# Graph attention and expert layers: part of the second stage's preparation moved into the attention's last slots

## What is computed

```
# x: 16 x 1024 x 256, adj: 16 x 1024 x 1024
Wh = layernorm(x) @ W.T;  e = leaky_relu(Wh@a1 [i] + Wh@a2 [j], 0.2), -inf where adj == 0
x1 = x + softmax(e) @ Wh
n  = layernorm(x1)
w  = softmax(mean_over_batch(n) @ Wr + br)          # per node, 8 experts
h  = relu(bn(n @ W1[e] + b1));  h = relu(bn(h @ W2[e] + b2))
out = x1 + sum_e w[:, e] * (h @ Wo[e] + bo[e])
```

## Time and profile before

| | us |
|---|---|
| median of 3 runs | 2882.55 (2881.88 to 2883.1) |
| the profiled execution | 2883.41 |
| its span, first to last instruction | 2881.6 |
| PE busy | 2809.0 (97%) |
| DVE busy | 2415.4 (84%) |
| ACT busy | 2133.3 (74%) |
| POOL busy | 685.5 (24%) |
| mean granted TensorE clock | 0.991 of full |

### The profile page before, as it was taken

One profiled execution on the slowest core, in us unless ns is written; L12 is line 12 of the kernel. 1 busy time (PEld: TensorE's weight loads), 2 busy tenths in 40 slices (PEclk: granted clock), 3 DMA queues, 4 the chain that ended last, 5 costly groups with the idle time before them and its releaser, 6 DMA issues.

```text
span 2881.6 us, 48960 instructions
## 1 busy us (share of the span) xinstructions
PE 2809.0 (97%) x17110; PEld 2482.4 (86%) x17110; DVE 2415.4 (84%) x3560; ACT 2133.3 (74%) x3035; POOL 685.5 (24%) x953
## 2 busy tenths in 40 slices
PE   7999999998999999999999999999999999999998
PEld 7989989988788888888888888888888888888887
DVE  7999999997688888888888888888888888888887
ACT  6889889887676777776777677677777777667775
POOL 5888888887000000000000000000000000000000
PEclk9999999999899999999999999999999999999999
DMA  4444444443344454554454444455455445544554
GB/s 144 158 154 149 154 154 155 148 158 110 105 172 151 159 161 159 159 165 156 157 163 159 154 159 163 148 168 162 151 168 161 154 158 162 161 152 160 157 156 136
DMA packets 159980, 445.25 MB, mean 155 GB/s; under 512 B 16016, under 2 KB 73784, under 8 KB 159808
## 3 DMA queue, kind: packets, MB, share of 16 engines
q1 hardware_dynamic: 159808, 442.96, 47.7%
HBM read 401.97 MB, written 40.93 MB: 154 GB/s over the span
## 4 chain that ended last, share of the span: by engine, by line
PE 73%; ACT 1%; DVE 1%; issue 0%; DMA 0%; ACTq 0%; DVEq 0%
PE z_ps L52 17%; PE z_ps L53 16%; PE z_ps L54 16%; PE m_ps L1012 7%; PE m_ps L1014 7%; PE m_ps L1015 7%; PE turn_ps L987 1%; PE turn_ps L995 1%; ACT h L1143 0%; PE m_ps L1029 0%; DVE h_lo L1304 0%; DVE h_sums L1311 0%; DMA gate_row<-w_scratch 0%; DVE h_lo L1316 0%; PE turn_ps L1103 0%
## 5 line engine op out<-in xcount | busy, mean ns | idle before, releaser
L1143 ACT ACTIVATE h<-z_ps,bn_shift,bn_scale 128x512 f32<-128x512 f32 x1024 | 748.5, 774 | 557.2 <-PE z_ps L54 333.2
L1304 DVE TENSOR_TENSOR h_lo<-h_sums,h_hi 128x1792 fp32r<-128x1792 f32 x256 | 519.4, 2029 | 208.5 <-ACT h_hi L1157 208.4
L1012 PE MATMUL m_ps<-h_hi,wo_ops 128*128 128x256 f32 x1792 | 513.3, 286 | 4.0 <-DVE h_lo L1304 4.0
L1015 PE MATMUL m_ps<-h_hi,wo_ops 128*128 128x256 f32 x1792 | 502.9, 281 | 0.0
L1014 PE MATMUL m_ps<-h_lo,wo_ops 128*128 128x256 f32 x1792 | 502.6, 280 | 0.0
L1157 ACT ACTIVATE h_hi<-h_sums 128x1792 fp32r<-128x1792 f32 x256 | 434.8, 1698 | 62.6 <-DVE h_sums L1327 59.9
L86 POOL TENSOR_TENSOR ffn_vareps<-ffn_mv,ln_eps 128x4 f32<-128x4 f32 x32 | 7.2, 224 | 1899.1 <-DVE ffn_mv L80 1899.1
L1311 DVE TENSOR_TENSOR h_sums<-h,gate_row 128x1024 f32<-128x1024 f32 x256 | 313.8, 1226 | 124.5 <-ACT h L1143 110.1
L52 PE MATMUL z_ps<-h_hi,w_hi 128*128 128x512 f32 x1024 | 405.8, 396 | 6.9 <-DVE h_lo L1316 6.9
L52 PE MATMUL z_ps<-xT_hi,w_hi 128*128 128x512 f32 x1024 | 407.7, 398 | 2.7 <-ACT h L1143 2.0
L53 PE MATMUL z_ps<-xT_lo,w_hi 128*128 128x512 f32 x1024 | 405.9, 396 | 0.0
(11 more groups left out here) (152 smaller groups left out, 5481.0 us busy)
## 6 DMA issues: line engine op xcount, KB each, us to landing
wo_ops<-wo_scratch SPq DMA_DIRECT2D x248, 896.0 KB, 6.3
adj_sb<-in_adj SPq DMA_DIRECT2D x128, 512.0 KB, 3.5
gate_row<-w_scratch SPq DMA_DIRECT2D x256, 256.0 KB, 4.5
x_sb<-in_x SPq DMA_DIRECT2D x64, 256.0 KB, 2.8
x_scratch<-x_sb SPq DMA_DIRECT2D x128, 128.0 KB, 1.8
ffn_x<-x_scratch SPq DMA_DIRECT2D x32, 512.0 KB, 7.5
out<-ffn_x SPq DMA_DIRECT2D x31, 512.0 KB, 8.0
...
```

What stands on the lines that cost most here:

```text
L1012: pe.matmul(m_at(q), w_hi, x_hi[:, x, :], start=e == 0 and q in OPENERS, stop=False, skip_group_check=True)
L1015: done = pe.matmul(m_at(q), w_lo, x_hi[:, x, :], start=False, stop=e == E - 1, skip_group_check=True)
L1143: return act.activation(dst, src, ACT.Relu, bias=bn_shift[layer][:, col], scale=bn_scale[layer][:, col])
L1304: dve.tensor_tensor(h2_lo[s % 2][:, :, :], g2[:, 1:8, :], bits(h2_hi[s % 2][:, :, :]), ALU.subtract) \
```

## The change

- Two Wo experts are loaded by SP in slot 8 of the last pair, ahead of the first tile's load. Their sums (DVE, slot 13) and expert 0's rounding and remainder are made in slots 13 and 14.
- Slot 12 (`GATE_SLOT`): TensorE transposes half of `node_table` (nodes 0 to 511) and the first row tile, ahead of the products of block 14; ACT copies and rounds them. Slot 14: logits of this half, z1(0), the softmax, the turned gates, ACT's copy, SP's store.
- The second half of the gates is made in the second stage: transposes at its start, logits between the layer groups of slot -2, softmax in DVE slots 0 and 1, `transpose_weights` at the end of PE slot 1, ACT's copy at the start of slot 2.
- The bias table comes in four parts, two matmuls each, in slots 4 to 7; `residual` moves to slots 9, 10, 14 and 15 for the first two tiles, and to slots 6 and 7 of its own tile afterwards (4 and 5 of the tile before, until now).
- Normalising of the second tile moves to slots 0 and 1, its transposes to 2 and 3. Experts 2 and on are summed and rounded in slots 0 and on.
- Buffers are shared to make room: wh, x and PSUM banks of the attention are read on by the second stage.

The diff, cut to this; `LastWeights` and `Gates` hold the old weight_sums, weight_upper, weight_lower and softmax as methods:

```diff
...
+        self.sums = [shared.x_rows[:, i * 4:(i + 1) * 4, :].rearrange("p s (h d) -> p (s h) d", d=P) for i in range(2)]
...
+    def home(self, e):
+
+        return (0, 0) if e == 0 else ((1, 2, 3)[(e - 1) % 3], (e - 1) // 3)
+
+    def load(self, sp, e):
+        i, _ = self.home(e)
+        for m in range(self.KB):
+            sp.dma_start(self.sums[i][:, (1 - m):4:2, :],
+                         self.Wo[e].rearrange("(k p) d -> p k d", p=P)[:, :, m * P:(m + 1) * P]) \
...
+    GATE_SLOT = UT - 4
...
+                if last and u == TB:
+                    sp.wait_ge(S["x1_ready"], (PAIRS - 1) * UT + TB)
+                    for e in range(2):
+                        last_w.load(sp, e)
...
+            sp.wait_ge(gates.wT_ready, 1)
+            sp.dma_start(w_dram[:, 0, :], first_tile.wT[0:E, :]).then_inc(first_tile.w_stored, DMA)
...
+                if last_pair and u == GATE_SLOT:
+                    pe.wait_ge(S["n1_added"], PAIRS * UT - CT + 1)
+                    pe.wait_ge(S["pT_lo_ready"], PAIRS * UT - 1)
+                    gates.transpose_rows(pe, lambda it, d: pT_ps[0][:, it * KB + d, :], feat_sum[:, 0:CT, :], ident)
+                    pe.wait_ge(norm.xn_ready, 1)
+                    for d in range(KB):
+                        for t in range(CT):
+                            last = pe.transpose(head_ps[:, d, t * P:(t + 1) * P], norm.xn[:, t, d * P:(d + 1) * P],
+                                                ident[:, :])
+                        last.then_inc(first_tile.xT_psum, 1)
...
+                if last_pair and u == GATE_SLOT + 2:
+                    pe.wait_ge(gates.featT_ready, 1)
+                    for it in range(CT):
+                        gates.row_logits(pe, pT_ps[0][:, 0, it * E:(it + 1) * E], gate_featT, wr_sb, it, it == CT - 1)
+                    pe.wait_ge(first_tile.xT_lo_ready, KB)
+                    pe.wait_ge(S["w12_lo_ready"], 1)
+                    for m in range(KB):
...
+                            last = split_matmul(pe, head_ps[:, m, :], w12_hi[:, 0, 0, at], w12_lo[:, 0, 0, at],
+                                                first_tile.xT_hi[:, d, :], first_tile.xT_lo[:, d, :], d == 0, d == KB - 1)
+                        last.then_inc(first_tile.z1_ready, 1)
+                    gates.transpose_weights(pe, pT_ps[0][0:E, CT:TB, :].rearrange("e t c -> e (t c)"), ident)
...
+                if last and u == GATE_SLOT:
+                    act.wait_ge(gates.featT_psum, 1)
+                    act.activation(gate_featT, pT_ps[0][:, :, :].rearrange("p (t k) c -> p t (k c)", k=KB), ACT.Copy,
...
+                    for d in range(KB):
+                        act.wait_ge(first_tile.xT_psum, d + 1)
+                        act.activation(first_tile.xT_hi[:, d, :], head_ps[:, d, :], ACT.Copy) \
+                            .then_inc(first_tile.xT_hi_ready, 1)
+                if last and u == GATE_SLOT + 1:
+                    last_w.upper(act, 0)
+                if last and u == GATE_SLOT + 2:
+                    gates.exponentials(act)
+                    act.wait_ge(gates.wT_psum, 1)
+                    act.activation(first_tile.wT[0:E, :], pT_ps[0][0:E, CT:TB, :].rearrange("e t c -> e (t c)"),
+                                   ACT.Copy).then_inc(gates.wT_ready, 1)
...
+                if last and u == GATE_SLOT + 1:
+                    for d in range(KB):
+                        dve.wait_ge(first_tile.xT_hi_ready, d + 1)
+                        dve.tensor_tensor(first_tile.xT_lo[:, d, :], head_ps[:, d, :], bits(first_tile.xT_hi[:, d, :]),
+                                          ALU.subtract).then_inc(first_tile.xT_lo_ready, 1)
+                    for e in range(2):
+                        last_w.add_blocks(dve, e)
+                if last and u == GATE_SLOT + 2:
+                    gates.centre(dve, pT_ps[0][:, 0, 0:CT * E].rearrange("p (t e) -> p t e", e=E))
+                    gates.weights(dve)
+                    last_w.lower(dve, 0)
...
+            return (1 if u == 2 + d else None) if 0 <= u < E else t if u >= 0 else None
...
+                    if s == E:
+                        sp.wait_ge(first_tile.w_stored, 2 * DMA)
                     load_gate(s)
-
-            for e in range(2):
-                load_sums(e)
+                if u == 1:
+                    sp.wait_ge(gates.wT_ready, 1)
+                    sp.dma_start(w_dram[:, 1, :], wT_sb[:, BANK:]).then_inc(first_tile.w_stored, DMA)
+                    sp.dma_start(wT_sb[:, 0:BANK], w_dram[:, 0, :]).then_inc(wT_in, DMA)
+
+            sp.wait_ge(first_tile.w_stored, DMA)
+            for s in range(2):
+                load_gate(s)
...
+            def gate_bias(q):
+
+                if q == 0:
+                    pe.wait_ge(wT_in, DMA)
+                    pe.wait_ge(S["xT_lo_ready"], 4)
+                    pe.wait_ge(gates.wT_ready, 1)
+                else:
+                    pe.wait_ge(S["table_ready"], q)
+                for i in range(2):
+                    it = 2 * q + i
+                    last = pe.matmul(turn_ps[:, 0, i * D:(i + 1) * D], wT_sb[:, it * P:(it + 1) * P], bo_sb[:, :],
+                                     start=i == 0, stop=True, skip_group_check=True)
                 last.then_inc(S["table_psum"], 1)
...
+                    if s == 0:
+                        pe.wait_ge(gates.featT_ready, 1)
+                        row_logits(0)
...
                 if u == -2:
-                    transpose_gate()
-                if u == -1:
-                    gate_bias()
+                    row_logits(1)
+                for q in range(CT):
+                    if u == 4 + q:
+                        gate_bias(q)
...
                         pe.wait_ge(norm.xn_ready, t + 1)
+                        if t == 1:
+                            pe.wait_ge(gates.wT_ready, 1)
+                        if t == 2:
+                            pe.wait_ge(S["table_ready"], CT)
...
+                    if u == -2:
+                        row_logits(3)
+                if u == 1:
+                    gates.transpose_weights(pe, turn_ps[0:E, 0, :], ident)
+
+            gates.transpose_rows(pe, lambda it, d: m_ps[:, it // 2, (it % 2 * KB + d) * P:(it % 2 * KB + d + 1) * P],
+                                 node_table[:, CT:TB, :], ident)
...
+                if u == 2:
+                    copy_gate()
                 first_relu(u + Z1 - 1, 1)
+                if u < 0:
+                    first_upper(u + Z1 - 1)
...
+                if u >= 0:
+                    first_upper(u + Z1 - 1)
+                if u == 1:
+                    gates.exponentials(act)
+                if 0 <= u - 4 < CT:
+                    copy_gate_bias(u - 4)
...
-                if 2 <= u + 2 < E and u >= 0:
+                    if u == i:
+                        normalise(1, i)
+                if 1 <= u + 2 < E:
                     weight_upper(u + 2)
...
+                wait(dve, S["table_ready"], t * 2 + half + 1 if t < CH else 0)
...
-                if u == -2:
-                    for e in range(2):
-                        weight_sums(e + 2)
-                        weight_lower(e)
-                if 4 <= u + 2 < E:
-                    weight_sums(u + 2)
+                if u < 0:
+                    first_lower(u + Z1 - 1)
+                if 2 <= u + 2 < E:
+                    last_w.add_blocks(dve, u + 2)
...
-                    if t is not None and u >= 0:
+                    t = rows_due(u - 1, i)
+                    if t is not None:
...
-                    t = tile_due(u, 4 + i, 1)
+                    t = tile_due(u, 1 + i, -1) if u < 2 * E else tile_due(u, 6 + i, 0)
                     if t is not None and u >= 0:
                         residual(t, i)
+                    if u == E + 6 + i:
+                        residual(1, i)
...
+                if u == 0:
+                    norm.statistics(dve, x1_sb[1], x1_in[1], 1)
...
+                if 1 <= u + 1 < E:
+                    last_w.lower(dve, u + 1)
                 if u == 0:
-                    dve.wait_ge(S["table_ready"], 1)
-                    for i in range(2):
-                        residual(0, i)
+                    gates.centre(dve, turn_ps[:, 0, 0:CT * E].rearrange("p (t e) -> p t e", e=E))
+                if u == 1:
+                    gates.weights(dve)
+
+            dve.wait_ge(gates.featT_psum, 1)
+            dve.tensor_scalar(featT.rearrange("p t c -> p (t c)"), m_ps[:, 0:2, :].rearrange("p k c -> p (k c)"),
+                              float(D) ** 0.5 / B, None, ALU.mult).then_inc(gates.featT_ready, 1)
...
```

339 lines of the change are left out of this document (171 added, 168 removed).

## The result

The changed kernel takes **2852.32 us** (median of 4 runs, 2851.21 to 2853.97) beside 2882.72 of the kernel before in the same job (2881.88 to 2883.1, 4 runs): ratio 0.9895, 95% interval 0.9883 to 0.9907. That is 30.4 us faster, where 11.7 were forecast, and outside the range of 2865 to 2877. The profiled execution took 2852.83 us with a span of 2851.0 us, so the two spans to compare are 2881.6 and 2851.0, a difference of 30.6.

The account below looks back on a forecast made before the run. TensorE was taken as full from 834 us on, leaving only the seam between stages to gain. Terms 2.5 - 25.2 + 6.6 + 1.4 + 2.0 + 1.0 = -11.7 us turned 2882.55 into 2870.8 us, range 2865 to 2877.

Parts of the forecast that it names:

- 68.00 of 68.00 after y(8): Sign of being right: after product y(8), TensorE is still busy in every microsecond of a tile.
- In later tiles ... 0: Later tiles: the two residual additions move from slots 4 and 5 to 6 and 7, where DVE has slack: 0.
- First tile's load: Load of the second stage's first rows, behind four Wo loads on SP: just in time, 0, at worst 1 us.
- Seam: Attention's end: 16 added transposes and later x1 delay the second stage's start from 715.78 to about 718.3: +2.5 us.
- that rival: Gates not hidden: z1(0) and softmax run after the POOL chain, seam at 723, 2875.7 or the time of before; chance 0.07 for the latter.
- Start to y(0): Second stage's start to first last-layer product: six layer groups remain, 21.2 us for 46.45: -25.2 us.
- the clock term: Clock dips at the seam and in slots 0 and 1: one group at half speed, +2.0 us.
- y(0) to y(2): Slots 0 and 1: waits for relus (2.5 us) and second gate half's weights (2.8) make 23.5 of 16.94 us: +6.6 us.
- The POOL meeting: A POOL addition meeting a DVE subtraction, at the seam or before ACT's shift: 0 to 4 us, taken as +1.0 us.
- y(2) to y(8): First tile's following steps: four bias-table pieces, 2.9 us in all, half of it taken: +1.4 us.
- The rival of two dips of two groups each: The clock takes more: +8 instead of +2 us, 2876.8 at the worst, 2875.5 where one meets a wait; chance 0.13.
- The rival of the loop that takes everything back: Slots 0 to 7: ACT and DVE waits stretch each slot, deciding from 11.5 us; at 12.5 each, 2891 us; chance 0.05.

Follow-up runs that it names:

- a_resid: The changed kernel with the two residual additions of later tiles back in slots 4 and 5 of the tile before, from tile 3 on: 2850.80 us.
- b_pad640: The kernel before with only 640 unused bytes per partition ahead of xT_hi, moving operands to multiples of 256 bytes: 2860.92 us.
- a_norm1: The changed kernel with both of ACT's normalising operations of tile 1 in slot 1 instead of one each in slots 0 and 1: 2848.51 us.
- b_w128: The kernel before with only the layer weights w12 moved from 192 to 128 above a multiple of 256 bytes: 2859.93 us, one run.
- b_w12: The kernel before with only the layer weights w12 moved from 192 above a multiple of 256 bytes to a multiple: 2878.10 us, one run.
- a_best_w: a_best with the layer weights w12 also moved by 64 bytes to a multiple of 256: 2843.67 us.
- a_best: The changed kernel with even tiles' xT at a multiple of 256 bytes, wo_ops kept at 224, and both normalising operations of tile 1 in slot 1: 2847.46 us.

## Why the prediction was wrong

**The step that failed** is in the first paragraph: "68.00 of 68.00. Nothing of the work there can go away by reordering." The sentence is true, and it was used for more than it says. Busy all the time means that no gap shows; it doesn't mean that the pace is fixed. From it the sum put 0 on 248 later steps, and the diff's new allocation of buffers, which stands in plain sight in `FirstTile`, got no term, no bound and no rival. The runs showed the later steps 18.8 us of span shorter by the balance above (17.1 by the two medians), since the new addresses took 0.04 us off most layer groups. The sign that the prediction named for this stretch, 68.00 of 68.00 after y(8), came true and couldn't tell. The words "In later tiles ... 0" were right for what they spoke of, the residual additions (a_resid).

Point by point, up to y(8):

- *First tile's load*: charged 0. The load went out at 688.47, and its reader waited 0.20 us. Right.

```profile
692.58 1.41 DVE L73 BATCH_NORM_STATS2 ffn_stats<-ffn_x 128x6 f32<-128x256 f32 x4 [0.20 <-DMA ffn_x<-x_scratch]
```

- *Seam*: +1.5 on this axis against +2.5. It can't be read closer: the kernel before and b_pad640, the same up to there, start their second stage at 715.78 and 714.26, and the kernels with the changed order between 715.5 and 719.7. z1(0) ran ahead of the barrier (711.94 to 714.98), and the gates were hidden; that rival is gone.
- *Start to y(0)*: 22.98 us against 21.2. The order and the small waits (0.52 and 1.06 us for relus) were as worked out. The difference is mostly z1(1), 4.05 us (718.54 to 722.59) instead of 2.8, since the clock is 0.50 in the window 718 to 720; that is the group which the clock term had charged separately.
- *y(0) to y(2)*: +8.9 against +6.6. z1(4) waited 1.16 us for relus, which wasn't worked out. The POOL meeting of the earlier trace rows happened ahead of the shift that ACT waits for (1.99 us under 2.02), but it cost more than the one microsecond that was taken. z1(5) waited 4.66 us where 2.5 were worked out, and then ran at half clock, 5.3 us instead of 2.8. The wait for the gate weights, worked out as 2.8, was 0.17, because the longer wait ahead covered it; with the first gone (a_norm1) it is 2.59. So each chain was real, and one wait hid the other.
- *y(2) to y(8)*: +1.2 against +1.4. A bias piece took 1.1 us, 4.4 in all, over the 2.9 that were taken and inside the bounds; less of it reached the path.
- *Clock*: two dips, z1(1) and z1(5), 1.3 + 2.5 us, against one group at +2.0. So the term was too small by nearly half. The rival of two dips of two groups each overstated them, and its price was misread from the rows: in the kernel before, z1(1) behind the tiny matmuls took 4.4 us, z2(1) behind the wait of 6.53 took 4.5, z1(3) behind the bias table 4.8, and the groups right behind the first and the last of these were back at 2.80. That is one group a dip. By the page "TensorE: Matmul & The Clock Gate" of the Trainium skill, Part 4, transposes don't count as busy, and z1(1) and z2(0) would both have been slow; the trace has z1(1) slow, and z2(0), from 722.59 on, at 1.00: agreement with half of it. The kernel before had already spoken against it: z1(0), the first group behind its 24 transposes, took 3.10 us (720.79 to 723.89), and only its first matmul was slow.
- The rival of the loop that takes everything back: from y(2) to y(8) the slots took 8.1 to 9.3 us, far from its 11.5.

The Trainium skill ("SBUF — State Buffer", Who interferes with whom) lists two SBUF read ports of TensorE, one for the moving operand and one for weight loads, and calls them independent. Read that way, no distance between the two operands should matter. b_w128 differs: moving the weights alone, from distance 192 to 128, brought a group from 2.80 to between 2.72 and 2.75 us. The measurement decides; whether the two ports meet or something else does, no run here shows. The same section's rule, that only the ports shared by DVE and GpSimd lead to waiting on one another, agrees with the POOL operation that takes 0.20 us alone and 1.99 us under a DVE operation with two SBUF inputs.

What stays open: why some distances are long, why the same distances (192 and 192) gave 2.73 and 2.76, and what sets the products' 2.50 to 2.56 us. A contention with other engines' accesses wasn't told apart from one between TensorE's own two operands, since the padding moved buffers of DVE and ACT along with them; only the runs that move the weights (b_w12, b_w128, and a_best_w against a_best) keep every other distance.
